# Ranked node tiles in a graph network: 36 of them are finished within the attention passes

## What is computed

```
edge_index = stack([src, dst])
h = relu(layernorm(x)); x = x + L0(h)   # filter sum per edge, sum of x[dst]*f over src, softplus MLP, batch norm
h = relu(layernorm(x)); x = x + L1(h)   # two one-head attention layers, self loops, each y = x + att, then layer norm
h = relu(layernorm(x)); x = x + L2(h)   # message MLP with edge_attr, mean over dst, update MLP, layer norm
h = relu(layernorm(x)); x = x + L3(h)   # attention with 8 heads of 16, self loops

# one attention layer
h = x @ W;  logit = leaky_relu(a_src[src] + a_dst[dst], 0.2)
e = exp(logit - max);  alpha = e / segment_sum(e, dst)
att = segment_sum(h[src] * alpha[:, None], dst) + bias
```

## Time and profile before

| What | us |
|---|---|
| median of the three runs | 6766.14 |
| profiled execution | 6757.42 |
| its span | 6755.7 |
| setup until the first scatter | 194.5 |
| scatters of the setup | 194.5 to 1197.4 |
| `layer0_dst_pass` | 1224.2 to 2219.7 |
| src pass, softplus, first product | 2219.7 to 2528.8 |
| one-head pass 0 | 2528.8 to 3504.9 |
| gap F: end of layer l = 0, product for l = 1 | 3504.9 to 3572.7 |
| one-head pass 1 | 3572.7 to 4548.6 |
| gap H: end of l = 1, norm, product for messages | 4548.6 to 4644.3 |
| message pass | 4644.3 to 5620.5 |
| update, norm, product | 5620.5 to 5740.9 |
| 8-head pass | 5740.9 to 6719.0 |
| output | 6719.0 to 6755.7 |

### The profile page before, as it was taken

How to read it: one execution, slowest core, us unless ns; L and a number is a source line. 1 busy time by engine, 2 the same in 40 slices (tenths; PEclk the granted TensorE clock), 3 DMA queues, 4 the chain that set the end, 5 groups by cost and what they waited for, 6 DMA issues and landing times. The chain is left out here.

```text
span 6755.7 us, 70389 instructions
## 1 busy us (share of the span) xinstructions
PE 3366.4 (50%) x17726; PEld 2923.7 (43%) x17726; DVE 3206.9 (47%) x10050; ACT 1571.4 (23%) x3893; POOL 4738.0 (70%) x4985
## 2 busy tenths in 40 slices
PE   5444301455544773455533455544477776255554
PEld 2222101455543762444432444444476664244443
DVE  8999711333332462333344433336244436465555
ACT  6000000222211671322222322223122224000000
POOL 3677777677777737777756777775777774777775
PEclk8555555667766885666666666666687777566665
DMA  2233333455543744444434444443354542455444
GB/s 73 82 120 118 108 117 104 152 174 173 175 155 134 246 146 122 146 141 145 142 94 123 147 145 142 145 117 117 105 156 145 151 144 73 126 150 145 147 144 117
DMA packets 494348, 913.25 MB, mean 135 GB/s; under 512 B 207337, under 2 KB 242624, under 8 KB 493699
## 3 DMA queue, kind: packets, MB, share of 16 engines
q1 hardware_dynamic: 343814, 617.78, 27.2%
q0 software_dynamic: 150144, 290.98, 16.3%
HBM read 663.11 MB, written 245.25 MB: 134 GB/s over the span
## 5 line engine op out<-in xcount | busy, mean ns | idle before, releaser
L1929 POOL DMA_INDIRECT edge_buf<-node_table,ixr x1472 | 1391.1, 945 | 483.3 <-issue 445.5
L1929 POOL DMA_INDIRECT Y<-node_table,ixr x1460 | 1378.1, 944 | 444.9 <-issue 444.3
L1529 DVE TENSOR_TENSOR ACC<-ACC,bank 128x129 f32 (+3 forms) x3320 | 965.2, 291 | 620.7 <-issue 116.1
L559 POOL DMA_INDIRECT edge_records<-edge_buf x782 | 753.2, 963 | 259.6 <-issue 236.1
L2202 PE MATMUL bank<-adc,turned_buf 128*128 x2199 | 298.2, 194 | 1253.0 <-DVE z L2131 765.3
L2202 PEld LDWEIGHTS bank<-adc,turned_buf 128*128 128x128 bf16 x2199 | 223.0, 102 | 1366.8 <-issue 1318.5
L1503 PE MATMUL bank<-Y 128*128 128x129 f32 (+3 forms) x2920 | 665.0, 418 | 231.3 <-DVE ACC L1529 171.0
L1503 PEld LDWEIGHTS bank<-Y 128*128 128x128 f32 x2920 | 621.3, 320 | 252.7 <-issue 244.2
L1503 PE MATMUL bank<-edge_buf,Y 128*128 128x129 f32 (+3 forms) x2944 | 639.9, 404 | 163.1 <-DVE ACC L1529 95.0
L1503 PEld LDWEIGHTS bank<-edge_buf,Y 128*128 128x128 f32 x2944 | 598.0, 306 | 181.0 <-issue 180.1
L2125 DVE TENSOR_REDUCE pk<-bank 128x16 f32<-128x48 f32 (+1 forms) x276 | 89.1, 323 | 1086.8 <-DMA edge_buf<-node_table,ixr 631.6
(11 more groups left out here) (400 smaller groups left out, 5786.3 us busy)
## 6 DMA issues: line engine op xcount, KB each, us to landing
Y<-onehots SPq DMA_DIRECT2D x368, 512.0 KB, 3.7
turned_buf<-onehots_turned SPq DMA_DIRECT2D x276, 256.0 KB
layer_messages<-ACC SPq DMA_DIRECT2D x28, 2112.0 KB
edge_buf<-edge_records SPq DMA_DIRECT2D x191, 288.0 KB, 3.3
onehots<-Y SPq DMA_DIRECT2D x105, 512.0 KB, 3.6
XI<-layer_messages SPq DMA_DIRECT2D x84, 528.0 KB, 4.7
onehots_turned<-turned_buf SPq DMA_DIRECT2D x105, 256.0 KB, 2.0
zone_oh<-onehots SPq DMA_DIRECT2D x52, 512.0 KB, 4.0
```

What stands on the lines that cost most here:

```text
L559: pool.indirect_dma_start(rec_d, bass.IndirectOffsetOnAxis(ap=ixs[h][:, j:j + 1], axis=0), rec[h][:, j, :], None) \
L1529: nc.vector.tensor_tensor(acc, acc, self.places.at(k, j, self.w), ALU.add).then_inc(self.added, 1)
L1929: pool.indirect_dma_start(ring[q][:, j, 0:w], None, table, bass.IndirectOffsetOnAxis(ap=ixr[q][:, j:j + 1], axis=0)).then_inc(rows_in[q], 16)
```

## The change

1. The setup ranks the node tiles by their number of edges, the smallest first, and the edge tiles are laid out in that order. `node_at` holds where a rank's tile lies, `moved` by how much a tile's number changes. x is loaded tile by tile by `node_at`, on SP among the rounds of scatters.
2. So the edges of the first ranks are summed early. From half 48 on, every three halves a group of three tiles (`FT` = 3, 12 groups, `EARLY` = 36 tiles) is taken through steps in consecutive halves: reciprocal, division on ACT, add and statistics, root on ACT, norm on ACT, turn, multiply, add, store. For l = 0 this goes up to the next layer's table, for l = 1 up to the message table, in the 8-head pass up to the output. The work behind a pass is for 14 tiles (4 groups), the output's in three parts with one DMA a tile on SP and ACT.
3. The zone halves of a GAT pass come after every second regular half from 22, and one-head passes use `one_set`; the banks that this frees are used for the finishing.
4. The records hold source numbers, so these are mapped to ranks within `layer0_dst_pass`: `label_sources`, in three parts, 50 steps each, four steps in a half, each of them two DVE operations. SP loads the fields of the last 14 halves once more at half 64.
5. In `node_product` branches that no call used are gone, and a first group can be given.

```
+FT = 3
+EARLY_GROUPS = 12
+EARLY = FT * EARLY_GROUPS
+FIRST_LATE = EARLY // GN
+FINISH_AT = [48 + 3 * f for f in range(EARLY_GROUPS)]
...
+                        st.then(v.scalar_tensor_tensor(size_row[0:NB2, :], bank[2][0:NB2, 0:NB2], 64.0, late_row[0:NB2, :], ALU.mult, ALU.add))
+                        st.then(v.scalar_tensor_tensor(size_col[0:NB2, :], bank[5][0:NB2, 0:1], 64.0, late_col[0:NB2, :], ALU.mult, ALU.add))
...
+                        st.then(v.tensor_scalar(smaller[0:NB2, :], size_row[0:NB2, :], size_col[0:NB2, :], None, ALU.is_gt))
...
+            late_from, late_loaded_after = 78, 64
+            label_parts = ((0, 31, 32), (31, 62, 62), (62, REG_HALVES, 78))
...
+                        if half == ("regular", late_loaded_after):
+                            for n in range(late_from, REG_HALVES):
+                                sp.dma_start(late_fields[:, (n - late_from) * G:(n - late_from) * G + G, :],
+                                             rec_v[n].rearrange("p (j w) -> p j w", j=G)[:, :, EA:RW]).then_inc(late_in, 16)
...
+                        elif step <= by_rank:
+                            b = step - 1
+                            label_then(v.tensor_scalar(move, key, iota_row[:, b:b + 1], moved[:, b:b + 1], ALU.is_equal, ALU.mult))
+                            label_then(v.tensor_tensor(label[:, 0:count], label[:, 0:count], move, ALU.add))
...
+                    label_steps_each, label_steps_all = 4, by_rank + 2
+
+                    def label_sources(i):
+
+                        for n, (lo, hi, after) in enumerate(label_parts):
+                            first = (i - after) * label_steps_each
+                            for step in range(max(first, 0), min(first + label_steps_each, label_steps_all)):
+                                label_step(n, step)
...
                         (finish_regular if kind == "regular" else finish_zone)(k, i)
+                        if kind == "regular":
+                            label_sources(i)
...
-                    nc.vector.tensor_copy(src_ix[:, 0:ZONE_AT].unsqueeze(2), fields[:, :, R_SRC - EA:R_SRC - EA + 1])
-                    nc.vector.tensor_copy(src_ix[:, ZONE_AT:NT].unsqueeze(2), zone_fields[:, :, R_SRC - EA:R_SRC - EA + 1])
...
+            places = one_set if heads == 1 else two_sets
...
-            order = Order(("pick", 2, 1, IH), ("weights", weighed_after, 1, 1 if heads > 1 else 0), ("zone", 22, 5, IH))
+            order = Order(("pick", 2, 1, IH), ("weights", weighed_after, 1, 1 if heads > 1 else 0), ("zone", 22, 2, IH))
...
-            sums_of = Sums(order, two_sets, sums[0], summed_w, added)
+            sums_of = Sums(order, places, sums[0], summed_w, added)
...
+                    def store_nodes(f):
+
+                        sp.wait_ge(nodes_taken, f + 1)
+                        sp.sem_inc(spt, 1)
+                        if finish == "to output":
+                            for t in range(f * FT, f * FT + FT):
+                                sp.dma_start(out[bass.ds(node_row(mybir.EngineType.SP, t), P), :], X[:, t, :]).then_inc(nodes_stored, 16)
...
+                    def finish_nodes(f, step):
+
+                        v, at = nc.vector, early(f)
+                        if step == 0:
...
+                            then(v.reciprocal(by_head(den, heads)[:, at, :], weights))
+                            dve.sem_inc(node_weights, 1)
...
+                        elif step == 1:
+                            dve.wait_ge(nodes_scaled, f + 1)
+                            then(v.tensor_tensor(ACC[:, at, 0:D], by_tile(scaled_psum, P), XI[:, at, :], ALU.add))
+                            count_nodes(f, ACC[:, :, 0:D])
+                        elif step == 2:
+                            norm_nodes(f, f + 1 if finish == "to attention" else 2 * f + 1)
...
-                    for b in range(NBP):
+                    for b in range(EARLY, NBP):
                         ins = v.scalar_tensor_tensor(Y[:, b, :], ACC[:, b, 0:D], den[:, b:b + 1], XI[:, b, :], ALU.mult, ALU.add)
```

More of the change, by code:

```diff
@@ L126, in then, with halves_of_ranks, finishing @@
         self.eng.wait_ge(self.sem, self.start + self.n)
+def halves_of_ranks(n):
+    return -(-(-(-(E // P) * n // FULL)) // G)
+assert all(FINISH_AT[f] >= halves_of_ranks((f + 1) * FT) for f in range(EARLY_GROUPS))
+def finishing(n):
+    return [(f, n - FINISH_AT[f]) for f in range(EARLY_GROUPS) if FINISH_AT[f] <= n]
 def later(i):
@@ L1114, in take_product, with node_product @@
                 for q in range(tiles_of(g) // 2):
-                    dve.wait_ge(prod, 2 * g + q + 1)
+                    dve.wait_ge(prod, 2 * (g - first) + q + 1)
                     after(v, then, slice(g * GN + 2 * q, g * GN + 2 * q + 2), product_psum(g, q, cols))
             dve.sem_inc(taken, 1)
-        def node_product(src, w, after, before=None, normed=None, cols=D, store=None, keep=None, reduce_ahead=False):
-            norm_done, ready, turned, turned_sb, prod, taken, steps, stored = (
-                sem(n) for n in ("norm_done", "ready", "turned", "turned_sb", "prod", "taken", "steps", "stored"))
-            dve_copies = normed is not None and before is None
+        def node_product(src, w, after, normed, cols=D, store=None, keep=None, reduce_ahead=False, first=0):
+            norm_done, turned, turned_sb, prod, taken, steps, stored = (
+                sem(n) for n in ("norm_done", "turned", "turned_sb", "prod", "taken", "steps", "stored"))
             def turned_at(g):
@@ L2142, in half @@
                             ask_zone_weights()
+                        for f, step in finishing(n):
+                            finish_nodes(f, step)
                     for n in range(HALVES):
@@ L2457, in after @@
                     then(v.tensor_copy(ad[:, at, :], rows_psum[:, :, D + heads:cols]))
-            node_product(XI, wx[l], after, before, normed, cols=cols, store=(table, H, D + heads), reduce_ahead=l == 2)
+            node_product(XI, wx[l], after, normed, cols=cols, store=(table, H, D + heads), reduce_ahead=l == 2, first=first)
         def add_row(v, then, t, row, op=ALU.add):
@@ L2524, in _ @@
                 def _(act):
-                    for g in range(NG):
+                    for g in range(first, NG):
                         scaled(g, ACT.Identity, t).then_inc(norm_done, 1)
@@ L2661, in _ @@
                     weights_of_nodes(nc.vector, then, 8)
-                    for n in range(4):
+                    for n in range(len(parts)):
                         finish(dve, nc.vector, then, n)
```

491 lines of the change are left out of this document (357 added, 134 removed).

## The result

The changed kernel takes 6827.77 us (median of 4 runs, 6824.93 to 6829.57), the kernel before on the same chip 6765.86 (median of 4 runs). The ratio is 1.0089, 95% interval 1.0076 to 1.0102: 62 us slower, where 62.5 were forecast. The profiled execution has a span of 6824.6 us, 68.9 more than that of the kernel before; it took 1.4 us less than its median, the one before 8.4 less than its own.

| Stage | before | after | difference | predicted |
|---|---|---|---|---|
| until the setup's first scatter | 194.5 | 199.1 | +4.6 | +4.3 |
| dst pass | 995.5 | 1069.7 | +74.2 | +80.6 (labels 72.6, clock 5, loads 3) |
| one-head pass 0 | 976.1 | 1010.7 | +34.6 | +30 |
| gap F | 67.8 | 39.1 | -28.7 | -30.6 |
| one-head pass 1 | 975.9 | 1012.2 | +36.3 | +30 |

What follows compares the result with a forecast made beforehand. POOL's 782 indirect DMAs bound every edge stage, leaving time in the gaps. Terms -82.4 + 4.3 + 72.6 + 5 + 3 + 60 = +62.5 on 6757.4 give 6819.9, median 8.7 above: 6828 us; range 6785 to 6870.

Steps and rivals of the forecast that it cites:

- labels: Dst pass: mapping source numbers to ranks on DVE between scale and next one-hot lengthens the loop, +72.6 us (49 to 90).
- clock: Dst pass: longer waits may lower PE's granted clock, 0.68 before, +5 us (0 to 20).
- loads: Dst pass: fourteen more loads on SP at half 64, ahead of that half's stores, +3 us (0 to 8).
- gap F: Stage after one-head pass 0, 67.8 us before: less divide, statistics and product work, gain 30.6 us (27 to 32).
- part 1: Dst pass, rank mapping beside halves 32 to 44: 50 pairs of DVE operations paid in full, 44.9 us.
- The loop: One-head passes, zone sum to zone sum: 23.3 to 24.2 us against POOL's 20.0, 11 times; +30 us a pass.
- Gap H: Stage after one-head pass 1, 95.7 us before: gain 39.7 us (32 to 41), 12.4 of it at POOL's flags.
- One set of banks at the passes' end: Gaps F and H: the last half's sum waits for the adds before it, 1.6 us lost in each.
- Setup and output: Setup: 21 more small DVE operations before the first scatter, +4.3 us; output: shorter reciprocal and parts, gain 12.1.
- the rivals: No one-head stall 0.16 (6745 to 6786 us); deeper stall 0.12 (6880 to 6930); labels hidden 0.10 (6688 to 6748).
- the forecast's own case: Time is paid in both the dst pass and the one-head passes: chance 0.62, range 6785 to 6870 us.
- the rule weighed ahead of the run: Dst pass: GpSimd stands still during DVE's tensor_scalar; 48 in the third part add up to 20 us, sum +82.

Runs made afterwards that it cites:

- the three kernels built from the one before: Kernel before with one set of PSUM banks in one-head passes (6759.29 us), with zone halves after every second regular half (6753.29), and with both (6839.25).
- two moves of order and a finer wait: Changed kernel with label steps ahead of the scale, zone load one half later, sums waiting bank by bank for adds: 6666.78 us, ratio 0.9869.

## Why the prediction was right, and where it was not

**The labels**. Forecast 72.6 us for them and 8 for clock and loads; 74.0 by the run without them. That a piece between scale and one-hot is serial, though DVE idles 4 us in every half, was the step that decided the sign, and moving the piece by one place shows it. The pair took 0.41 + 0.42 and 0.07 to 0.08 of steps, as taken from rows of other widths; there are 48 pairs in a part, not 50, since the first and the last of the 50 steps copy and convert. By part: POOL's waits from half 35 to 46 come to 48 us, those from half 64 to 72 to 29, none behind (forecast 44.9, 27.7, 0, on top of what it waited before). Forecast as "some 3.5 a half", most of part 1's wait came in three pieces of 8 to 13 us, at the zone halves: the sum was right, its place in time was not. In halves 67 to 69 a half took 13.0 to 13.5 us rather than 11.4, because the scaling of the zone rows (2.08 us, L1764) stands in the same place; I had not counted that. The terms for clock and loads were not there: the granted clock is 0.67 against 0.68, and the run without labels kept the loads and lost nothing.

**The one-head passes**. Forecast 30 each, 27 to 38; measured 34.6 and 36.3. The loop was drawn right: turned load behind zone load, 5.09 us for PE, period 23.6 to 24.2 us (from one of POOL's waits to the next) against a forecast 23.3 to 24.2. That both conditions are needed is shown by the three kernels built from the one before. A loop was 3.6 to 4.2 us late, in the upper part of the 3.3 to 4.2 forecast, while the 30 taken allow some 3.5 for each of 11; nine waits showed, 33 and 34 us beyond the issue time in all. The finishing work was hidden as forecast: no wait behind half 49, and with the sums waiting by bank the passes take 976.1 and 975.9 us, as before the change, with all the finishing in them.

**Gap H**. Here the prediction's step was wrong, and the error hid in a sum that came out. It said that before the change the stage ends with POOL's flags at 4573.93 and that DVE would have been done 4 us earlier. In fact DVE divided until 4573.76, and its statistics and the norm's small operations went on to 4586.55: the flags were never last. The rows of the kernel before:

```profile
4560.55 13.21 DVE L2594 SCALAR_TENSOR_TENSOR Y<-ACC,den,XI 128x128 f32<-128x128 f32 x50 [0.16 <-DVE inv_deg L2591]
4573.80 9.77 DVE L240 BATCH_NORM_STATS2 stats<-Y 128x6 f32<-128x128 f32 x50
...
4586.34 0.21 DVE L255 SCALAR_TENSOR_TENSOR shift<-mean,var 128x50 f32<-128x50 f32 x1
```

What I had was an estimate for the changed kernel, in which flags at their old 7.80 us would have ended after DVE, told as if it were of the kernel before. The changed kernel shows:

```profile
4686.40 3.76 DVE L2893 SCALAR_TENSOR_TENSOR Y<-ACC,den,XI 128x128 f32<-128x128 f32 x14 [0.16 <-DVE inv_deg L2890]
4690.20 2.81 DVE L261 BATCH_NORM_STATS2 stats<-Y 128x6 f32<-128x128 f32 x14
4692.16 0.30 POOL L2904 TENSOR_TENSOR has_edge<-ACC,inv_deg 128x50 f32<-128x50 f32 x1 [19.57 <-issue]
```

The flags take 0.30 us and end before DVE does. So the stage from the first reciprocal to the shift fell from 27.4 us (4559.19 to 4586.55) to 10.2, a gain of 17.2 where 12.4 stood; norm and product gained 15.6 and 13.9 (forecast 15.0 and 13.6), and the pass's last sums and adds took 2.1 more (forecast 1.6). It could have been seen ahead: divide and statistics of 50 tiles are 13.21 + 9.76 us, while the flags ended 13.5 us behind the reciprocal.

**One set of banks at the passes' end**. 1.6 us forecast, half of eight adds; measured 3.7 in gap F of the kernel with one set alone, and 1.0 in its gap H. In that gap F the last eight adds start 1.4 us later behind the pass's end than before (4.6 against 3.2), and the five behind them 6.0 us after these instead of 3.8, since the last sum waits for all eight. The 2.1 above the forecast are about what gap F gained less, 28.7 for 30.6.

**Setup and output**: +4.6 for +4.3; -13.6 for -12.1. The last part was ready 17.6 us behind the pass's end, as in the sum; its last issue ended 2.1 us later, where three of 0.9 stood, and the landing took 3.5 us, where 4.3 were left for it. Issues with an address from a register took 0.80 us each (six in 4.80).

The total was nearer than its terms: labels, clock and loads were 6.4 too dear, gap H 5.0 too low in gain, the one-head passes 10.9 too cheap, F and the output within 2. In the profiles the difference is 68.9 us against 62.5, a miss of 6.4. That the medians differ by 61.9, almost the number forecast, is luck: the forecast laid the old median's distance from its profile, 8.7 us, on the new kernel too, whose median lay only 1.4 above. Of the rivals, none held beside the forecast's own case. With labels ahead of the scale, beside POOL's transfers, the dst pass stayed at 996.3 us, and POOL's 782 transfers took 749.6 us of busy time, 748.8 without any labels. By the rule weighed ahead of the run, that of the Trainium skill on the shared port ("SBUF — State Buffer", section "Who interferes with whom"), POOL could have stood still during 144 TENSOR_SCALARs of 0.41 us; no run here shows that.

## What to carry over

Idle time of an engine is room for work only in the place in its queue where it waits: behind the wait's end, ahead of what the other engine waits for, the same work is paid in full. Where several engines turn in a loop, count every step of the loop under the new rules, also those now hidden beside the longest one: taking the load out of the loop uncovered the zone half's adds. Work shifted under a transfer-bound pass is free only if it does not take away a second buffer or crowd one queue: here 87 us were won in the gaps and 145 lost in the passes, and two moves of order and a finer wait turned that into 88 us won.

## What was not expected of the hardware

POOL's flags, a TENSOR_TENSOR on 128x50 values, took 7.80 us before and 0.30 after. In both it starts 5.7 to 5.9 us after the reciprocal it waits for (4560.40 to 4566.13; 4686.25 to 4692.16); why so late is open. Before, it lay beside DVE's divide (a SCALAR_TENSOR_TENSOR with two operands in SBUF, x50, without a pause) and ended 0.17 us after it; after, the divide was over. The Trainium skill ("SBUF — State Buffer", section "Who interferes with whom") states that such a DVE instruction contends with a GpSimd instruction that reads SBUF; these rows agree. So do all eleven profiles: 7.68 to 7.97 us in the four with the divide of 50 tiles, each time ending 0.16 or 0.17 us after it, and 0.30 in the seven with one of 14, though no run was made to test this alone. POOL's indirect DMAs were hardly slowed by DVE's work: 751.73 us for 782 with labels beside them, 748.79 before.
